# Fewer address registers on VectorE's tile loop, a packed fill word, and a 34-column frame copy on ScalarE

## The reference, cut to what matters

```python
# x: (16, 768, 64, 64) float32; offset: (48, 2)
def _displace(x, offset):                       # 768 channels, 16 for each of 48 positions
    off_int = round(offset * 64); sub = offset * 64 - off_int
    shifted[c, y, x] = x[c, y - dy, x - dx]     # zero where it leaves the 64 x 64 image
    kern = exp(-(kx*kx + ky*ky) / 0.5); kern = kern / kern.sum()   # 3 x 3, moved by sub
    return depthwise_conv(shifted, kern, padding='SAME')
def _gn(v, G=32, eps=1e-5): ...                 # group norm: 24 channels x 64 x 64 to a group
x = x + _displace(_gn(x), offset)
```

## Time and profile before

| | us |
|---|---|
| median of 3 runs | 976.3 (976.01 to 976.35) |
| the profiled execution | 979.06 |
| its span, first to last instruction | 977.1 |
| VectorE busy | 824.8 (84%) |
| TensorE matmul busy | 785.6 (80%) |
| ScalarE busy | 638.9 (65%) |
| GpSimd busy | 368.1 (38%) |
| DMA | 403.09 MB, mean 413 GB/s |

### The profile page before, as it was taken

One profiled execution on the slowest core, in us unless ns is written; L12 is line 12 of the kernel. 1 busy time (PEld: TensorE's weight loads), 2 busy tenths in 40 slices (PEclk: granted clock), 3 DMA queues, 4 the chain that ended last, 5 costly groups with the idle time before them and its releaser, 6 DMA issues.

```text
span 977.1 us, 9088 instructions
## 1 busy us (share of the span) xinstructions
PE 785.6 (80%) x2132; PEld 383.6 (39%) x2132; DVE 824.8 (84%) x551; ACT 638.9 (65%) x461; POOL 368.1 (38%) x348
## 2 busy tenths in 40 slices
PE   0998987979979698897979879689797997979820
PEld 0544443434434343353434434345343443434410
DVE  7587988777798997978889899898998979797795
ACT  7778676564766747678466746577675785774661
POOL 0214034340432624013254393463845438250312
PEclk9999988989979799897998979989898897989955
DMA  9999999999999999999999999999999999999948
GB/s 364 427 401 423 392 405 429 429 429 428 430 429 430 432 428 414 430 429 430 431 429 406 398 433 376 407 419 393 431 408 430 430 427 431 431 431 430 430 208 343
DMA packets 27821, 403.09 MB, mean 413 GB/s; under 512 B 3216, under 2 KB 3216, under 8 KB 3216
## 3 DMA queue, kind: packets, MB, share of 16 engines
q1 hardware_dynamic: 27792, 402.71, 98.0%
HBM read 201.38 MB, written 201.33 MB: 412 GB/s over the span
## 4 chain that ended last, share of the span: by engine, by line
DVE 28%; DMA 27%; PE 20%; POOL 7%; issue 7%; ACT 5%; DVEq 3%; ACTq 2%; SPq 0%; POOLq 0%
PE sum_ps L289 17%; DMA out_dram<-xs 15%; DMA xs<-x_dram 12%; DVE xs L713 6%; DVE xs L716 6%; DVE smooth L709 6%; DVE smooth L704 6%; DVE xs L719 4%; POOL small L253 2%; POOL small L260 2%; ACT frame L417 2%; POOL small L257 2%; ACT unused L484 2%; POOL small L266 1%; ACTq L393 1%
## 5 line engine op out<-in xcount | busy, mean ns | idle before, releaser
L289 PE MATMUL sum_ps<-xs,bands 128*128 128x512 f32 x976 | 483.5, 653 | 51.2 <-DMA xs<-x_dram 51.2
L484 ACT ACTIVATE unused<-xs,small 128x4096 bf16 (+1 forms) x94 | 348.3, 3706 | 8.3 <-ACT small L470 4.8
L417 ACT ACTIVATE frame<-xs,small (+1 forms) x96 | 223.3, 2326 | 184.3 <-DVE smooth L709 183.3
L289 PEld LDWEIGHTS sum_ps<-xs,bands 128*128 128x128 f32 x976 | 200.6, 210 | 295.4 <-issue 282.2
L253 POOL TENSOR_TENSOR small<-small 128x3 f32<-128x3 f32 x32 | 41.6, 1299 | 570.6 <-ACT small L492 570.6
L289 PE MATMUL sum_ps<-xs,halves 128*128 128x512 f32 x496 | 230.0, 619 | 17.4 <-DMA xs<-x_dram 17.4
L704 DVE SCALAR_TENSOR_TENSOR smooth<-frame,side_w 128x612 f32 (+5 forms) x96 | 163.6, 1705 | 72.2 <-ACT frame L417 37.1
L713 DVE SCALAR_TENSOR_TENSOR xs<-smooth,small,xs 128x612 f32 (+5 forms) x96 | 163.5, 1703 | 51.9 <-POOL small L266 49.6
L709 DVE SCALAR_TENSOR_TENSOR smooth<-frame,side_w,smooth x96 | 159.7, 1664 | 7.5 <-DVE smooth L704 4.1
L719 DVE SCALAR_TENSOR_TENSOR xs<-smooth,small,xs 128x594 f32 (+9 forms) x96 | 159.8, 1664 | 3.4
L716 DVE SCALAR_TENSOR_TENSOR xs<-smooth,small,xs 128x594 f32 (+9 forms) x96 | 159.7, 1664 | 3.4
(11 more groups left out here) (132 smaller groups left out, 259.3 us busy)
## 6 DMA issues: line engine op xcount, KB each, us to landing
xs<-x_dram SPq DMA_DIRECT2D x96, 2048.0 KB, 14.8
out_dram<-xs SPq DMA_DIRECT2D x96, 2048.0 KB, 17.7
smooth<-offset_dram SPq DMA_DIRECT2D x1, 48.0 KB, 4.1
```

The lines of the kernel that those rows point to most:

```text
L289: last = nc.tensor.matmul(sum_ps[:, :], (FIRST, SAME, SECOND)[i], slot_px(n, c * BANK, (c + 1) * BANK), start=(i == 0 and c == 0), stop=(i ...
L417: nc.scalar.activation(frame[:, bass.ds(b, rows * PITCH)].rearrange("p (r c) -> p r c", c=PITCH)[:, :, LEFT:LEFT + W], xs[:, bass.ds(a, ro ...
L484: nc.scalar.activation(unused[:, :], xs[:, bass.ds(n % SLOTS * PIX, PIX)], ACT.Square, bias=neg_mean[:, i:i + 1], accum_out=squares[:, i:i ...
```

## The change

On VectorE: a fifth word for each tile, BESIDE, holds an address that the loop's head worked out from two others; the loop counts 1 to 96 and `side_w` has a column in front, so that no n + 1 is needed; `behind` and `turn` are worked out behind the register load, ahead of the second pass. In the setup, 12 small chained operations make the new fill word and 2 the fifth word. `fills` moves into the upper 64 partitions of `words`. On ScalarE: the fill word also has a first column, and there are six shapes: for shifts that leave at most 34 columns, 64 x 34 (in place of 64 or 50 rows of 64) or 34 x 34 (in place of 34 or 18 rows of 64).

```diff
-    WORDS = 4
-    KIND, TO, FROM, COLUMN = range(WORDS)
+    WORDS = 5
+    KIND, TO, FROM, BESIDE, COLUMN = range(WORDS)
+    NARROW = 2
+    COPIES = [(rows, W) for rows in SIDES] + [(SIDES[k], SIDES[NARROW]) for k in (0, NARROW)]
...
-                row = word & (1 << ROW_BITS) - 1
-                rows_kind = act.snap(word >> ROW_BITS)
+                column = word & (1 << COL_BITS) - 1
+                row = (word >> COL_BITS) & (1 << ROW_BITS) - 1
+                copy_kind = act.snap(word >> ROW_BITS + COL_BITS)
...
-                        xs[:, bass.ds(a, rows * W)].rearrange("p (r c) -> p r c", c=W),
+                        xs[:, bass.ds(a, rows * W)].rearrange("p (r c) -> p r c", c=W)[:, :, 0:cols],
...
-            chained(V.scalar_tensor_tensor(code[:, :, 0], kind[:, :, 1], float(1 << ROW_BITS), first_row[:, :, 1],
+            narrow, low, half = positive[:, :, 0], positive[:, :, 1], whole[:, :, 0]
+            chained(V.tensor_scalar(narrow, kind[:, :, 0], float(NARROW), None, ALU.is_ge))
+            chained(V.tensor_scalar(low, kind[:, :, 1], float(NARROW), float(len(SIDES)), ALU.is_ge, ALU.add))
...
                 dve.reg_load(next_tile, words[0:1, bass.ds(done * WORDS, WORDS)])
-                V.scalar_tensor_tensor(part, frame_window(behind, cols - 1), side_w[1][:, bass.ds(n, 1)], part,
+                turn = kind_of % 2
+                behind = (src + 1 - turn).with_bounds(min_val=1, max_val=most + 1)
+                part = smooth[:, bass.ds(turn.with_bounds(min_val=0, max_val=1), rows * cols)].rearrange(
+                    "p (r c) -> p r c", c=cols)[:, :, 0:cols - 1]
+                V.scalar_tensor_tensor(part, frame_window(behind, cols - 1), side_w[1][:, bass.ds(done, 1)], part,
...
-            def tile_of(n):
-                dve.reg_mov(done_count, n + 1)
-                done = dve.snap(done_count, min_val=1, max_val=TILES)
+            def tile_of(done):
+                dve.reg_mov(done_count, done)
                 kind_of = dve.snap(next_tile[KIND], min_val=0, max_val=2 * len(SIDES) ** 2 - 1)
-                dve.reg_mov(at_turn, kind_of & 1)
-                turn = dve.snap(at_turn, min_val=0, max_val=1)
...
-                dve.reg_mov(at_behind, src + 1 - turn)
-                dve.reg_mov(at_beside, src + 2 * turn - 1)
-                beside = dve.snap(at_beside, min_val=0, max_val=FRAME_ROWS * PITCH)
-                behind = dve.snap(at_behind, min_val=0, max_val=FRAME_ROWS * PITCH)
+                beside = dve.snap(next_tile[BESIDE], min_val=0, max_val=FRAME_ROWS * PITCH)
```

More of the change, by code:

```diff
@@ L104, in build @@
         base_w = xs[:, SLOTS * PIX:].rearrange("p (n k) -> p n k", k=3)
-        side_w = [sb(f"side_w{k}", [P, TILES]) for k in range(2)]
+        side_w = [sb(f"side_w{k}", [P, TILES + 1]) for k in range(2)]
         words = sb("words", [P, WORDS * (TILES + 1)], i32)
-        fills = sb("fills", [P, TILES], i32)
+        fills = words[HALF:P, 0:TILES]
         setup = smooth[:, 0:11 * 2 * POSITIONS].rearrange("p (n f a) -> p n f a", n=11, a=2)
@@ L680, in _, with smooth_tile @@
             V.engine_nop().then_inc(tile_done, 1)
-            next_tile = [dve.alloc_register(name) for name in ("next_kind", "next_to", "next_from", "next_column")]
+            next_tile = [dve.alloc_register(name) for name in
+                         ("next_kind", "next_to", "next_from", "next_beside", "next_column")]
             done_count = dve.alloc_register("done_count")
-            at_turn, at_beside, at_behind = (dve.alloc_register(name) for name in ("turn", "beside", "behind"))
-            def smooth_tile(rows, cols, src, beside, behind, turn, dst, n, done, weights):
+            def smooth_tile(rows, cols, src, beside, kind_of, most, dst, done, weights):
                 under = xs[:, bass.ds(dst, rows * W)]
@@ L741, in emit @@
                     smooth_tile(rows, cols, src.with_bounds(min_val=1, max_val=most),
-                                beside.with_bounds(min_val=0, max_val=most + 1),
-                                behind.with_bounds(min_val=1, max_val=most + 1), turn,
+                                beside.with_bounds(min_val=0, max_val=most + 1), kind_of, most,
                                 dst.with_bounds(min_val=0, max_val=(SLOTS - 1) * PIX + (H - rows) * W + W - cols),
-                                n, done, weights)
+                                done, weights)
                 choose(dve, kind_of, 0, len(SIDES) ** 2, emit, 2)
@@ L750, in _ @@
             dve.addr_align(256, max_nops=0)
-            with dve.Fori(0, TILES) as n:
+            with dve.Fori(1, TILES + 1) as n:
                 tile_of(n)
```

61 lines of the change are left out of this document (39 added, 22 removed).

## The result

The changed kernel is slower: 1015.12 us (median of 4 runs, 1011.7 to 1016.36) against 976.15 for the kernel before on the same chip, a ratio of 1.040 with a 95% interval of 1.0367 to 1.0432. The forecast was 968.6, with eight chances in ten from 964 to 976.3. The profiled execution took 1016.26 us, its span is 1014.5 (977.1 before), so the trace has to explain 37.4 us.

What follows compares the result with a forecast made beforehand. VectorE was taken to set the pace from 500 to 745 us, and loads elsewhere. Stretch 5.0, entry 2.15, around 370 0.7 and end 0.95, less setup 1.1, gave 7.7 us off 976.3: 968.6, eight in ten from 964 to 976.3.

Steps and rivals of the forecast that it cites:

- The step that failed: Load of the next tile's words, ahead of VectorE's second pass: a fifth register was put at no added time.
- the forecast's own use of it: At 200 ns a register, four tiles' second passes would lose a further 0.8 us, making the sum 6.9 instead of 7.7.
- The heads: VectorE's loop head ahead of first passes: 0.45 us shorter (bounds 0.45 and 0.52), 5.0 us over eleven tiles in 500 to 745.
- GpSimd's steps: Third-pass gaps at tiles 54 and 60: rise from 0.39 to 0.67 us, leaving 0.17 us gain each, 0.3 together.
- the rival rule: Whichever of VectorE and GpSimd starts first fully blocks the other; tiles 54 and 60 give nothing, sum 0.3 us smaller.
- The frame copies: ScalarE's copies ahead of tiles 46 and 47: 0.85 us shorter each, 1.7 us; with tile 48's head, 2.15 us earlier.
- The setup: Fourteen new operations before the loop: 3.35 us, first means 2.24 us later, 1.1 us lost (bounds 0 and 2.2).
- The sum: Whole kernel: 5.0 + 2.15 + 0.7 + 0.95 - 1.1 = 7.7 us less, giving 968.6 us.
- What it doesn't do: Words are not loaded behind the second pass; the load stays between passes, counted as certain and in the sum.
- the sign that I was wrong: 500 to 745 us stays at 410 GB/s, third-pass gaps grow past 0.7 us, or second passes of 900+ elements begin to wait.

Runs made afterwards that it cites:

- run 9: Kernel before plus two ladders of 72 register loads (1 to 8 words, places 0 to 3), ahead of VectorE's loop and after the last store, results used; one execution, 1105.32 us.
- run 11: Kernel before plus groups of 16 register loads behind the last store, while tiles are stored again, loaded, or both; one execution, 1131.2 us.
- run 1: Kernel before with its row of words begun one word (4 bytes) later, nothing else changed; 1012.53 us against 977.28, ratio 1.0366.
- run 3: Packed kernel: kernel after with the column packed into the KIND word, one load of four registers; 975.01 us against 976.25 for the kernel before, ratio 0.9984.
- run 8: Kernel with packed words, its load of the next tile's words moved behind the second pass; 974.67 us against 977.37 for the kernel before, ratio 0.9979.
- run 9's first version: Kernel before plus the same ladder of register loads, which the compiler removed as unused, so the work of the kernel before; 975.4 us.
- run 5: Copies alone: kernel before with only ScalarE's narrow frame copies and their 13 set-up instructions, VectorE's loop and words unchanged; 976.95 us against 977.28, ratio 1.000.
- run 7: Kernel after with the load of the next tile's five words moved behind the second pass; 1049.95 us against 977.28 for the kernel before, ratio 1.0747.
- run 10: Kernel before plus groups of 16 register loads behind the last store, at rest and while one engine at a time works; one execution, 1114.33 us.

## Why the prediction was wrong, point by point

**The step that failed** is this one: "The load now fetches five registers. ScalarE's load of one register has the same median of 0.59 us as VectorE's of four, and the minima differ by 66 ns, so I put the fifth at nothing." The rows were right: one register and four had cost the same because both were one read. What decides is how many reads a load falls into, and that goes by place before number: five words take 0.62 us from a multiple of 16 bytes and 1.18 from the next place. The fifth register took every tile's words off their multiple of 16 bytes, but for one in four: at rest 1.18 us in place of 0.36 (run 9), under stores 4.75 in place of 1.06 (run 11). One word's shift alone costs 35.3 us (1012.53 - 977.28, run 1), and packed words give all the loss back (run 3). The figure on the Trainium skill's page, 200 ns a register, which I had weighed and set aside, stands closer to the ladder, though it is given for another memory; but by the forecast's own use of it (0.8 us more on four tiles) it too would have missed. What it lacked were the stores, which make each read about three times as long (run 11), and the tiles that pay: not four of 612 elements, but 61 of the 72 with a first pass under 2 us, and 6 above.

**The heads.** Right in mechanism and size. Tile 52 waits 0.67 in place of 1.18, tile 71 0.38 in place of 0.89; 0.51 each, near the upper bound of 0.45 to 0.52. The group that stays takes 0.189 us, where I had taken 0.215. From tile 48's start to tile 71's end the first passes' gaps add to 12.57 us before and 7.25 with packed words.

**GpSimd's steps.** Tile 54's gap went from 0.39 to 0.67, as forecast. Its first pass waits 0.51 us less (0.44 in place of 0.95), like the other heads: by the profile it started at 582.23, while GpSimd's L259 ran from 580.94 to 582.51, and did not wait for it. So far as the profile's rough spans of GpSimd tell, the rival rule, by which this tile would give nothing, does not fit here. In the packed kernel such gaps are 0.81, and those of tiles 51 and 57 grew from 0.40 and 0.39 to 0.53. There the whole stretch of tiles 48 to 71 takes 241.14 us against 244.14, 3.0 less where I had summed 5.0; in the kernel of run 8 it is 239.75, 4.4 less. The difference is the third passes' 1.5 and, in the packed kernel, the second's 0.6.

**The frame copies.** Right in the length of a copy: those ahead of tiles 46 and 47 take 1.28 us in place of 2.11 (1.26 with the copies alone). What VectorE gains by them was put too high. With the copies alone tile 47 ends at 497.26 in place of 500.11, but most of these 2.85 us lie between executions and not in the change: run 9's first version, which did the same work as the kernel before, ends it at 497.73. Counted from the start of the square ahead of tile 46's copy to the start of tile 48, the kernel before takes 19.79 us (481.24 to 501.03), the copies alone 19.17 and the packed kernel 18.47. That is 0.62 less where 1.7 was forecast, and 1.32 less where copies and tile 48's head should have given 2.15. A shorter copy uncovers the loop head behind it (run 5), so the two savings do not add up in full.

**The setup.** The first whole-tile sum came at 22.68, forecast 22.6. Tile 0 ends 2.3 us later (43.68 against 41.34), and the same in the packed kernel, where 0.9 is left at tile 23.

**The sum, words apart.** Packed kernel and run 8 stand for the change without its loads: 1.2 and 2.7 us less, where the sum said 7.7. The spans say more (971.9 and 972.5 against 977.1), but that profiled execution of before was itself 2.8 us above its median. Run 9's first version shows what is left: its span is 973.6 and its stretch of tiles 48 to 71 takes 244.76 us. So the gain in the stretch stands (241.14; 418 GB/s over 500 to 745, inside the forecast's 417 to 422), but the packed kernel enters it only 0.5 us earlier, and ends tile 71 4.2 us and tile 95 2.4 us earlier. The lead is partly lost again behind tile 71; which wait takes it was not looked into. So the forecast would have been 5 to 6.5 us too low even with the words in place.

**What it doesn't do.** The diff leaves the load between the passes, as I had said. That load was named as the place that pays, and a wait at second passes of 900 elements and more as the sign that I was wrong. Its price was off by some 40 us (1015.12 against 975.01 with packed words).

Open: why the load of five words is longer on average behind the second pass than ahead of it (run 7), how stores and VectorE's pass act together, and whether the stores alone make up the long loads of the loop.

## What to carry to other kernels

Ask of a load of registers how many reads it falls into: keep the words of one turn in full groups of four at a multiple of 16 bytes, and pack small numbers into one word before adding a fifth. A duration that is the same for one and for four of something may be the price of a group, so look for its edge before adding one more; a range from 0.34 to 1.34 us for one instruction is a question to settle first, since what stretches one read stretches each of five. And where a wait moves between passes, add up the idle time ahead of each pass before and after: here 105.8 us of new waits cost 35, as the rest only took the place of old ones.

## What the runs showed of the hardware

- A register load reads four words from a multiple of 16 bytes at once (0.36 us) and others one by one, 0.31 for the first and 0.22 for each further one; two or three from such a place count as others (0.54, 0.76). Eight take 0.61 or 1.85 us by their place alone.
- Tiles being stored make each read 1.04 us in place of 0.32. Tiles being loaded at 433 GB/s do not, nor, with no transfer under way, does work of VectorE, ScalarE, GpSimd or TensorE, nor ScalarE's own register loads (278 ns each in run 10, with VectorE's unchanged at 1.18).
- The register load holds its engine's sequencer: nothing behind it issues until it is back. At tile 17 of the kernel after it runs from 200.1 for 4.6 us, and the operations behind it, which use none of its words, start at 204.7; this is the 4.60 us ahead of the second pass.
